# Spreading two small columns along rows: TensorE transposes, or a store and a broadcast load through DRAM

## The chip, the cores and the metric

The kernel runs on one core of one Trainium2 chip. The metric is the device time of one launch in microseconds (us); lower is better. The inputs and the output are those of the reference, in float32.

## What is computed

A decoder layer in three blocks, each followed by a layer norm: self-attention, a slot-attention block with a GRU cell, and a mixture of experts. The change lies in the second block. Its reference, cut down:

```python
# slots: (8, 256, 256), P: (8, 120, 256); k_proj, v_proj come from rmsnorm(P)
for _ in range(3):
    sn = slots * rsqrt(mean(slots * slots, axis=-1) + 1e-6) * w
    scores = einsum('bkd,bmd->bkm', sn @ Wq.T, k_proj) * D ** -0.5
    attn = softmax(scores, axis=-2)                      # over the 256 slots
    attn = attn / (sum(attn, axis=-1) + 1e-6)            # over the 120 context rows
    updates = einsum('bkm,bmd->bkd', attn, v_proj)
    slots = gru_cell(updates, slots, ...)
```

Two numbers per slot matter here: the **root** (the reciprocal root mean square of the slot, which scales its scores) and the **reciprocal of the column sum** (one over the sum of the slot's 120 attention weights).

## The kernel before

**Tiling.** There are 2048 slots in four groups of 512 (GT). Three iterations over four groups make STEPS = 12 steps, and each step handles one group. Slots lie transposed in SBUF, features on partitions and slots along the free dimension. Scores and attention weights have the 120 context rows on partitions and the 512 slots along the row. A step n has two halves, ch = 0 and 1, for the two 128-feature chunks of the hidden state.

**Why anything is spread.** Both per-slot numbers are made by matmuls with one output column (`squares`, L416, from the squared slots; `column_sums`, L1237, from the exponentials). They land as a 128x4 column block: slot t*128 + p on partition p, column t. They are used on 120 partitions with 512 slots along the row. `along_tokens` (L1210) does that turn: four TensorE transposes of a broadcast column against the identity put the 512 values on 120 partitions of a PSUM bank. `root_along(n)` (L1218) does it for the roots `rms` into bank 4, from which ScalarE copies them to `rr` (`rms_out`, L1362). `sums_along(n)` (L1249) does it for `crec` into bank 7, which VectorE reads directly.

**Order of the work.** It is written out by hand, one function per engine, and each engine runs its own list in order:

- TensorE (`slots_tensor`, L1217), for step n: r, z and n gates of half 0, then of half 1. A gate is six matmuls of 512 columns from the hidden state (`from_hidden`) and six of 256 columns from the update (`from_update`). The update of the r gate waits for the attention weights of the same step (`an_lo`). Between them stand `squares(n+2)` in `gates_n(n, 0)`, `column_sums(n+1)` in `gates_r(n, 1)`, and after `gates_z(n, 1)` the two spreads and `context_scores(n+2)`.
- ScalarE (`slots_scalar`, L1355): the tanh of the gates (`gate_r`, `gate_z`, `new`), `hidden_n`, `weights(n+1)` (the float16 copy of the attention weights), `rms_out(n+2)`, `squared_slots(n+3)`, `exponentials(n+2)`, `sums_high(n+3)`, `high_part(n+3)`.
- GpSimd (`slots_pool`, L1474): `slot_root(n+2)` (the power of -0.5), `difference` (old slots less candidate), `weights_low(n+1)`.
- VectorE (`slots_vector`, L1503), for step n: `reset(n,0)` L1553, `candidate(n,0)` L1561, `column_sums(n+1)` L1532 and L1536, `update(n,0)` L1568, `new_slots(n,0)` L1573, `weights(n+1)` L1546, `scaled_scores(n+2)` L1517, `reset(n,1)`, `candidate(n,1)`, `denominators(n+2)` L1527, `sums_low(n+3)` L1508, `low_part(n+3)` L441, `update(n,1)`, `mean_square(n+3)` L448, `new_slots(n,1)`.
- SyncE (`slots_sync`, L1451) issues nine loads at the start of the block and then nothing until the next block; it has no work while the steps run.

In step 10 the VectorE list differs: `weights(11)` stands before `update(10,0)`, behind four operations of the following layer norm (`norm_sum(0)`, L1085 to L1096).

Of the kernel before, what the change touches and what calls it, by code (L numbers as in the profile page):

```python
# [6 lines left out]
F32 = mybir.dt.float32  # L7
# [8 lines left out]
P = 128  # L16
# [18 lines left out]
def decoder_layer(nc, a, out):  # L35
# [23 lines left out]
    with top:  # L59
# [53 lines left out]
        PIECES = SHARED_PIECES + 4 * E  # L113
        halves = nc.dram_tensor("halves", [PIECES, P, 2 * I], F16, kind="Internal").ap()
# [257 lines left out]
        r_pow, rb_mm = sem("r_pow"), sem("rb_mm")  # L372
        h_hi, h_lo, h_sq, h_sum, ss_mm, r_msq = (sem(k) for k in ("h_hi", "h_lo", "h_sq", "h_sum", "ss_mm", "r_msq"))
# [3 lines left out]
        SQ_UP = 64.0  # L377

# [37 lines left out]
        def squares(n):  # L416
            if n < WHOLE:
                PE.wait_ge(h_sum, n + 1)
                if n == 0:
                    PE.wait_ge(vw_lo, 1)  # L420
                if n >= 1:
                    PE.wait_ge(r_msq, meaned(n - 1))
            else:
                PE.wait_ge(r_msq, squares_low(n))
                PE.wait_ge(h_sq, squares_high(n))
            if n >= 2:
                PE.wait_ge(c_eps2, n - 1)
# [29 lines left out]
        p_out = [sem(f"p_out{u}") for u in range(STAGED)]  # L457


        with ExitStack() as c:  # L460
# [20 lines left out]
            w_in = [sem(f"w_in{i}") for i in range(4)]  # L481
            x_in = [sem(f"x_in{i}") for i in range(3)]
# [700 lines left out]
        with ExitStack() as c:  # L1183
# [13 lines left out]
            warm_gelu = sb(c, "warm_gelu", [P, 1])[:, :]  # L1197
            tr_, tz, hn, t1, t2, nn, dl = (sb(c, k, [P, GT]) for k in ("tr_", "tz", "hn", "t1", "t2", "nn", "dl"))
# [11 lines left out]
            def along_tokens(bank, rows, column):  # L1210


                for t in range(TG):
                    mm = PE.transpose(ps[0:rows, bank, t * P:t * P + P], column[:, t:t + 1].broadcast_to((P, rows)), ident[:, :])
                return mm

            def slots_tensor():  # L1217
# [19 lines left out]
                def column_sums(n):  # L1237
                    PE.wait_ge(g_rec, n + 1)
                    if n + 1 < STEPS:
                        PE.wait_ge(r_msq, meaned(n + 1))  # L1240
                    if n >= 1:
                        PE.wait_ge(c_eps2, n)
                    for t in range(TG):
                        k = t * P // S
                        mm = PE.matmul(ps[:, 6, TG + t:TG + t + 1], exf[:, t * P:t * P + P], grec[0:M, k:k + 1],
                                       start=True, stop=True)
                    mm.then_inc(cs_mm, 1)

                def sums_along(n):  # L1249
                    PE.wait_ge(c_rec, n + 1)  # L1250
                    if n >= 1:
                        PE.wait_ge(an_out, BG * n)
# [17 lines left out]
                def gates_r(n, ch):  # L1270
# [8 lines left out]
                    if ch == 1 and n + 1 < STEPS:  # L1279
                        column_sums(n + 1)  # L1280
# [12 lines left out]
                def gates_n(n, ch):  # L1293
# [28 lines left out]
                for n in range(STEPS):  # L1322
# [3 lines left out]
                    if n == STEPS - 2:  # L1326
                        PE.wait_ge(rr_out, STEPS)
# [12 lines left out]
                    if n + 1 < STEPS:  # L1340
# [14 lines left out]
            def slots_scalar():  # L1355
# [67 lines left out]
                for n in range(STEPS):  # L1423
# [12 lines left out]
                    if n + 2 < STEPS:  # L1436
                        rms_out(n + 2)
# [13 lines left out]
            def slots_sync():  # L1451
# [10 lines left out]
                for q in range(SHARED_PIECES):  # L1462
                    SY.wait_ge(p_out[q % STAGED], 16 * (q // STAGED + 1))
                    SY.dma_start(sw_flat[:, 4 * I * (q // 2):4 * I * (q // 2 + 1)].rearrange("p (i c n) -> p i c n", i=2, c=2)[
                        :, :, q % 2, :], halves[q].rearrange("p (i n) -> p i n", i=2)).then_inc(sw_in, 16)

# [36 lines left out]
            def slots_vector():  # L1503
# [7 lines left out]
                def scaled_scores(n):  # L1511
                    VE.wait_ge(rr_out, n + 1)
# [16 lines left out]
                def column_sums(n):  # L1529

                    VE.wait_ge(cs_mm, n + 1)
                    VE.tensor_scalar(cse[:, :], ps[:, 6, TG:2 * TG], SUM_EPS, None, ALU.add).then_inc(c_eps2, 1)  # L1532
                    VE.wait_ge(c_eps2, n + 1)
                    if n >= 1:
                        VE.wait_ge(cb_mm, n)
# [108 lines left out]
        with ExitStack() as c:  # L1644
# [73 lines left out]
            gathered = [sem(f"gathered{q}") for q in range(NT // 2)]  # L1718
# [493 lines left out]
            def experts_tensor():  # L2212
# [49 lines left out]
                def add_sums():  # L2262

                    PE.wait_ge(made, 18)
                    for t in range(TG):
                        if t % CT == 0:
                            PE.wait_ge(gathered[(EARLY + t) // CT], 16)
# [153 lines left out]

            def combine_load(engine, q):

                rows = back_y[P + q * CT * P:P + (q + 1) * CT * P, :].rearrange("(t p) d -> p t d", p=P)
                engine.dma_start(xs[:, q * CT:(q + 1) * CT, :], rows).then_inc(gathered[q], 16)
# [25 lines left out]
            def combine_vector():  # L2451
                def statistics(tiles, done):
                    for t in tiles:
                        if t < EARLY and t % CT == 0:
                            VE.wait_ge(gathered[t // CT], 16)
# [82 lines left out]
```

## Time and profile before

| | |
|---|---|
| time, median of 3 runs (lowest to highest) | 886.9 us (886.7 to 887.6) |
| profiled execution, its own time | 890.64 us |
| span in that profile | 889.4 us |
| busy in the span: TensorE matmul, VectorE, ScalarE, GpSimd | 97%, 68%, 63%, 42% |
| granted TensorE clock, mean | 0.996 of full speed |
| attention block, slots block, experts | about 0 to 363 us, 363 to 560 us, 560 to 889 us |
| DMA traffic while the steps run (380 to 545 us) | at most 2 GB/s in the slices of 400 to 550 us |

The profile is one execution on the hardware profiler. Its time is 3.7 us above the median of the runs, so differences are worked out within it and then set against the median. "Busy" of TensorE is a modelled figure, since matmuls overlap; the start of each matmul is what to read. A row such as `dl<-slots,nn` names the written tile, then what is read.

### The profile page before, as it was taken

How to read it: one execution, taken by the hardware profiler on the slowest of the kernel's cores; microseconds unless marked ns; L12 is line 12 of the kernel's file. 1: busy time of each engine (PE TensorE's matmuls, PEld its weight loads, DVE VectorE, ACT ScalarE, POOL GpSimd, SP SyncE). 2: the span in 40 equal slices, each digit the busy share in tenths (PEclk: the TensorE clock that was granted, in tenths of full speed). 3: DMA queues.
4: the chain of work that ended last, by engine and by line, in shares of the span. 5: the costliest groups of instructions: out<-in, count | busy, mean ns of one | idle time of the engine just before them, and what ended most of it. 6: DMA issues, size and time to landing. Idle time of an engine off the chain costs nothing. (4 is left out here: it accounts for less than half of the span.)

```text
span 889.4 us, 23089 instructions
## 1 busy us (share of the span) xinstructions
PE 859.9 (97%) x8094; PEld 680.0 (76%) x8094; DVE 606.1 (68%) x1669; ACT 557.2 (63%) x1251; POOL 377.8 (42%) x492
## 2 busy tenths in 40 slices
PE   5999999999999999999999999999999999999996
PEld 3888788888888888767676666676788888887864
DVE  3667588776667675756666667869677767766655
ACT  4988776777676776655756565564455555555555
POOL 1634354343433475324444332544534444444433
PEclk9999999999999999999999999999999999999999
DMA  9733424342424331410000000399423323333226
GB/s 317 207 126 113 142 97 152 119 160 96 143 94 138 103 119 49 62 42 2 1 1 1 2 1 1 105 393 356 158 52 50 49 44 50 49 50 50 43 27 195
DMA packets 61579, 88.04 MB, mean 99 GB/s; under 512 B 17279, under 2 KB 46527, under 8 KB 61343
## 3 DMA queue, kind: packets, MB, share of 16 engines
q1 hardware_dynamic: 53439, 75.52, 25.8%
q0 software_dynamic: 7488, 10.27, 7.3%
q8 instruction: 71, 1.16, 0.6%
q10 hardware_dynamic: 544, 0.79, 0.3%
q14 instruction: 37, 0.30, 0.1%
HBM read 56.00 MB, written 30.56 MB: 97 GB/s over the span
## 5 line engine op out<-in xcount | busy, mean ns | idle before, releaser
L648 POOL TENSOR_SCALAR prob<-prob,rden 128x128 f32<-128x128 f32 (+1 forms) x256 | 122.9, 498 | 183.1 <-DVE rden L949 183.0
L2219 PE MATMUL ps<-slots,e 128*128 128x128 f16 x1872 | 190.0, 219 | 2.2 <-DVE xs L2386 2.1
L2219 PEld LDWEIGHTS ps<-slots,e 128*128 x1872 | 152.6, 97 | 35.3 <-issue 4.4
L843 ACT ACTIVATE prob<-prob,nmx 128x128 f32<-128x128 f32 (+1 forms) x256 | 113.2, 444 | 29.8 <-DVE nmx L943 29.8
L2227 PE MATMUL ps<-e,xT 128*128 x312 | 117.3, 378 | 0.0
L2316 ACT ACTIVATE slots<-slots 128x512 f32<-128x512 f32 x78 | 49.1, 630 | 106.8 <-DVE slots L2370 106.8
L943 DVE CUSTOM_DVE_ANT_0 prob<-ps,mask 128x128 f32<-128x128 f32 (+1 forms) x256 | 73.7, 353 | 41.5 <-PE ps L730 41.5
L31 PE MATMUL ps<-xT,wqkv 128*128 128x256 f16 x768 | 97.2, 278 | 2.0 <-ACT slots L850 1.4
L31 PEld LDWEIGHTS ps<-xT,wqkv 128*128 128x128 f16 x768 | 73.4, 99 | 18.3 <-issue 6.9
L1731 POOL DMA_INDIRECT xg<-rows_x,dst x39 | 40.9, 1049 | 106.3 <-DVE mask L2359 103.0
L2228 PE MATMUL ps<-e,xT 128*128 x312 | 85.0, 273 | 0.0
L2375 DVE TENSOR_TENSOR xT<-slots,xT 128x1024 f16<-128x1024 f32 x39 | 47.8, 1225 | 39.9 <-ACT xT L2322 39.9
L2191 POOL DMA_INDIRECT back_y<-xs,dst x39 | 62.2, 1595 | 29.8 <-DMA back_y<-xs,dst 16.7
L2370 DVE SCALAR_TENSOR_TENSOR slots<-ps,b1e 128x512 f32<-128x512 f32 x78 | 53.7, 691 | 26.5 <-PE ps L2219 26.3
L592 DVE SCALAR_TENSOR_TENSOR parted<-piece,parted 128x256 f16<-128x256 f32 x144 | 59.8, 463 | 0.0
L31 PE MATMUL ps<-an,wqkv 120*128 120x256 f16 x432 | 58.9, 272 | 0.5 <-POOL an L1477 0.5
L730 PE MATMUL ps<-slots 64*128 64x128 f32 (+1 forms) x512 | 53.1, 345 | 2.5 <-ACT slots L850 2.5
L31 PEld LDWEIGHTS ps<-an,wqkv 120*128 120x128 f16 x432 | 41.2, 99 | 16.5 <-POOL an L1477 2.5
L31 PE MATMUL ps<-wst,whh 128*128 128x512 f16 x216 | 52.5, 379 | 0.0
L31 PE MATMUL ps<-s,whh 128*128 128x512 f16 x216 | 52.5, 379 | 0.0
L956 DVE COPY pT<-ps 128x768 f32<-128x768 f32 x32 | 30.6, 956 | 31.8 <-PE ps L700 31.8
L741 PEld LDWEIGHTS ps<-pT,v 128*64 128x64 f32 x768 | 42.4, 139 | 11.5 <-issue 11.5
(267 smaller groups left out, 1855.3 us busy)
## 6 DMA issues: line engine op xcount, KB each, us to landing
halves<-parted SPq DMA_DIRECT2D x36, 512.0 KB, 2.9
piece<-in_L_ffn_ew SPq DMA_DIRECT2D x32, 512.0 KB, 4.5
e<-halves SPq DMA_DIRECT2D x16, 1024.0 KB, 15.2
piece<-in_L_ffn_sh_w SPq DMA_DIRECT2D x4, 512.0 KB, 8.8
sw<-halves SPq DMA_DIRECT2D x4, 512.0 KB, 6.8
rows_x<-xs SPq DMA_DIRECT2D x4, 512.0 KB, 7.4
xs<-back_y SPq DMA_DIRECT2D x8, 256.0 KB, 4.4
out<-xs SPq DMA_DIRECT2D x8, 256.0 KB, 2.1
```

The costliest lines, as they stand in the source:

```text
L31: mm = pe.matmul(out, w, x, start=first and n == 0, stop=last and n == len(products) - 1, **kw)
L592: VE.scalar_tensor_tensor(share(piece_part(q, 1)), share(like_part(q)), WS, share(piece_part(q, 0)), ALU.mult, ALU.subtract).then_inc(p_lo, 1)
L648: PO.tensor_scalar(prob[u][:, h, r], prob[u][:, h, r], rden[u][:, h, t:t + 1], 1.0, ALU.mult, ALU.mult).then_inc(normed, 1)
L730: mm = PE.matmul(ps[:, 2 + 2 * p + h, query_tile(t)], qk[p][r, 0, t * P:t * P + P], qk[p][r, 1, 0:(t + 1) * P], start=True, stop=True)
L843: SC.activation(at, at, ACT.Exp, bias=nmx[u][:, h, t:t + 1], scale=-1.0, accum_out=den[u][:, h, t:t + 1]).then_inc(exped, 1)
L943: VE.tensor_tensor_reduce(prob[u][:, h, r], ps[:, 2 + h, r], mask[:, r], -SCALE, HIGHEST, ALU.add, ALU.min, nmx[u][:, h, t:t + 1]).then_in ...
L2191: PO.indirect_dma_start(back_y, bass.IndirectOffsetOnAxis(ap=dst[:, i:i + 1], axis=0), yo[i % 2], None, compute_op=ALU.add).then_inc(rows_ ...
L2219: yield PE.matmul(ps[:, 2 * u + q, (k % 4) * P:(k % 4) * P + P], w[ch][h], xgT[u][j][:, ch, :], start=n == 0, stop=n == 3 * DC - 1)
L2227: yield PE.matmul(ps[:, 4 + u, :], he[u][0][:, k, :], w, start=k == 0, stop=False, skip_group_check=True)
L2228: yield PE.matmul(ps[:, 4 + u, 0:D], he[u][1][:, k, :], w[:, 0:D], start=False, stop=k == IC - 1, skip_group_check=True)
L2316: SC.activation(z, z, ACT.Gelu_apprx_tanh).then_inc(U_gelu, 1)
L2370: VE.scalar_tensor_tensor(z, ps[:, 2 * u + q, :].rearrange("p (k t) -> p k t", k=4), 1 / WS, bias, ALU.mult, ALU.add).then_inc(U_bias, 1)
```

## The change

The first two roots and the first column sums are still turned by transposes (ROOTS_TURNED = 2, SUMS_TURNED = 1). The ten later roots (n = 2 to 11) and eleven later column sums (n = 1 to 11) go through DRAM: SyncE stores the 128x4 block into a row of 512 floats and, when that store has landed, loads the row back to 120 partitions at once (a broadcast load). VectorE then reads `rr` and the new tile `cb` from SBUF. So that each partition stores two neighbouring floats instead of four scattered ones, the slots are given to partitions in another way (`paired`): the weights of the one-column matmuls are read with a step of two elements. `column_sums(n+1)` moves from `gates_r(n, 1)` into `gates_n(n, 0)` on TensorE, ahead of `squares(n+2)`, and its result goes to bank 7. ScalarE's `rms_out(n+2)` goes away for n + 2 from 2 on. The combine loads of the last block use semaphores again that the first block had used, and wait for 32 instead of 16 where they do.

```diff
+        root_row = nc.dram_tensor("root_row", [GT], F32, kind="Internal").ap()
+        sums_row = nc.dram_tensor("sums_row", [GT], F32, kind="Internal").ap()
...
+        ROOTS_TURNED, SUMS_TURNED = 2, 1
+        def paired(t):
+            return t.rearrange("p (k q j) -> p k j q", k=BG, j=TG // BG)
...
                     for i in range(2):
-                        mm = PE.matmul(ps[:, 6, t:t + 1], sqh[i][:, t * P:t * P + P], one_h, start=i == 0,
+                        mm = PE.matmul(ps[:, 6, t:t + 1], paired(sqh[i][:, :])[:, t // BG, t % BG, :], one_h, start=i == 0,
...
         def slot_root(n):
             PO.wait_ge(r_msq, meaned(n))
-            if n >= 1:
+            if 1 <= n <= ROOTS_TURNED:
                 PO.wait_ge(rb_mm, n)
+            elif n > ROOTS_TURNED:
+                PO.wait_ge(root_put, 16 * (n - ROOTS_TURNED))
...
                 def column_sums(n):
                     PE.wait_ge(g_rec, n + 1)
...
                     for t in range(TG):
-                        k = t * P // S
-                        mm = PE.matmul(ps[:, 6, TG + t:TG + t + 1], exf[:, t * P:t * P + P], grec[0:M, k:k + 1],
-                                       start=True, stop=True)
+                        k = t // BG
+                        weights = exf[:, t * P:t * P + P] if n < SUMS_TURNED else paired(exf)[:, k, t % BG, :]
+                        mm = PE.matmul(sums_of(n)[:, t:t + 1], weights, grec[0:M, k:k + 1], start=True, stop=True)
...
                     from_hidden(n, 0, ch, False)
-                    if ch == 1 and n + 1 < STEPS:
-                        column_sums(n + 1)
                     PE.wait_ge(an_lo, n + 1)
...
                     from_hidden(n, 2, 2 * DC + ch, True).then_inc(hn_mm, 1)
+                    if ch == 0 and n + 1 < STEPS:
+                        column_sums(n + 1)
                     if ch == 0 and n + 2 < STEPS:
                         squares(n + 2)
...
-                    if n + 1 < STEPS:
-                        sums_along(n + 1)
                     if n + 2 < STEPS:
-                        root_along(n + 2)
                         context_scores(n + 2)
...
-                    if n + 2 < STEPS:
-                        rms_out(n + 2)
                     hidden_n(n, 1)
...
+                def token_pairs(row):
+                    return row.rearrange("(k q j) -> q k j", k=BG, j=TG // BG)
+                def put_sums(n):
+                    SY.wait_ge(c_rec, n + 1)
+                    if n > SUMS_TURNED:
+                        SY.wait_ge(sums_in, 16 * (n - SUMS_TURNED))
+                    SY.dma_start(token_pairs(sums_row), crec[:, :].rearrange("p (k j) -> p k j", k=BG)).then_inc(sums_put, 16)
...
+                def spread_sums(n):
+                    SY.wait_ge(sums_put, 16 * (n - SUMS_TURNED + 1))
+                    SY.wait_ge(an_out, BG * n)
+                    SY.dma_start(cb[0:M, :], sums_row.rearrange("(o t) -> o t", o=1).broadcast_to((M, GT))).then_inc(
+                        sums_in, 16)
...
+                for n in range(STEPS):
+                    if n + 1 < STEPS:
+                        put_sums(n + 1)
+                    if n + 2 < STEPS:
+                        put_root(n + 2)
+                    if n + 1 < STEPS:
+                        spread_sums(n + 1)
+                    if n + 2 < STEPS:
+                        spread_root(n + 2)
...
                 def weights(n):
-                    VE.wait_ge(cb_mm, n + 1)
+                    if n < SUMS_TURNED:
+                        VE.wait_ge(cb_mm, n + 1)
+                    else:
+                        VE.wait_ge(sums_in, 16 * (n - SUMS_TURNED + 1))
...
-                        VE.scalar_tensor_tensor(an[0:M, cols], ex[0:M, k, :], grec[0:M, k:k + 1], ps[0:M, 7, cols],
+                        VE.scalar_tensor_tensor(an[0:M, cols], ex[0:M, k, :], grec[0:M, k:k + 1],
+                                                ps[0:M, 7, cols] if n < SUMS_TURNED else cb[0:M, cols],
```

`put_root` and `spread_root` are built like `put_sums` and `spread_sums`, on `r_pow`, `root_in`, `root_put` and `sc_out`. VectorE's `scaled_scores(n)` waits for `root_in`, and its reciprocal L1536 for `sums_put` of the step before.

**How the instructions move.** TensorE in step 1 of the program before, from the column sums to the scores (`grec,ex` are the column sums of step 2, `ident,crec` and `ident,rms` the two spreads, `s,kq` the scores of step 3; `wst,whh` is a hidden-state gate, `an,wqkv` an update gate):

```order
806 L1245 MATMUL ps<-grec,ex 128x1 [waits c_eps2,r_msq,g_rec]
807 L1245 MATMUL ps<-grec,ex 128x1 x3
808 L31 MATMUL ps<-an,wqkv 128x256 [waits an_lo]
809 L31 MATMUL ps<-an,wqkv 128x256 x5
810 L31 MATMUL ps<-wst,whh 128x512 [waits tz_out]
811 L31 MATMUL ps<-wst,whh 128x512 x5
812 L31 MATMUL ps<-an,wqkv 128x256 x6
813 L1214 MATMUL ps<-ident,crec 120x128 [waits an_out,c_rec]
814 L1214 MATMUL ps<-ident,crec 120x128 x3
815 L1214 MATMUL ps<-ident,rms 120x128 [waits rr_out,r_pow]
816 L1214 MATMUL ps<-ident,rms 120x128 x3
817 L31 MATMUL ps<-s,kq 120x256 [waits sc_out,h_hi,h_lo]
818 L31 MATMUL ps<-s,kq 120x256 x11
```

In the changed program the column sums stand ahead of the squares (`one_f,sqs`), in the same step:

```order
796 L1264 MATMUL ps<-grec,ex 128x1 [waits c_eps2,g_rec]
797 L1264 MATMUL ps<-grec,ex 128x1 x3
798 L442 MATMUL ps<-one_f,sqs 128x1 [waits h_sq,r_msq]
799 L442 MATMUL ps<-one_f,sqs 128x1 x7
800 L31 MATMUL ps<-an,wqkv 128x256 [waits t2_out]
```

and the stretch from the update of the r gate to the next gate is:

```order
804 L31 MATMUL ps<-an,wqkv 128x256 [waits an_lo]
805 L31 MATMUL ps<-an,wqkv 128x256 x5
806 L31 MATMUL ps<-wst,whh 128x512 [waits tz_out]
807 L31 MATMUL ps<-wst,whh 128x512 x5
808 L31 MATMUL ps<-an,wqkv 128x256 x6
809 L31 MATMUL ps<-s,kq 120x256 [waits sc_out,h_hi,h_lo]
810 L31 MATMUL ps<-s,kq 120x256 x11
811 L31 MATMUL ps<-wst,whh 128x512 [waits hn_out]
```

The two spreads are gone between the z gate and the scores, and the column sums come one r gate earlier, right behind the hidden part of the n gate. SyncE's list behind the loads of the block, where the program before goes on with the stores and loads of the next block (`sums_row` and `root_row` are the two rows in DRAM):

```order
99 L1485 DMA sums_row<-crec 128x2x2 [waits c_rec]
100 L1491 DMA root_row<-rms 128x2x2 [waits r_pow]
101 L1496 DMA cb<-sums_row 120x512 [waits an_out,sums_put]
102 L1502 DMA rr<-root_row 120x512 [waits sc_out,root_put]
103 L1485 DMA sums_row<-crec 128x2x2 [waits sums_in,c_rec]
104 L1491 DMA root_row<-rms 128x2x2 [waits root_in,r_pow]
```

There are 42 such transfers, four per step and two in the last, each load behind its own store. VectorE's list keeps its order; only its waits change:

```order
917 L1583 TENSOR_SCALAR cse<-ps 128x4 [waits cs_mm]
918 L1589 RECIPROCAL crec<-cse 128x4 [waits sums_put,c_eps2]
919 L1625 SCALAR_TENSOR_TENSOR dl<-tz,dl 128x512 [waits tz_out,dl_out]
920 L1630 SCALAR_TENSOR_TENSOR slots<-dl,nn 128x512 [waits u_out]
921 L1602 SCALAR_TENSOR_TENSOR an<-ex,grec,cb 120x256 [waits an_hi,an_lo,g_rec,sums_in]
922 L1602 SCALAR_TENSOR_TENSOR an<-ex,grec,cb 120x256
923 L1568 ISA sc,gmx<-ps,rr 120x256 [waits g_exp,sc_mm,root_in]
```

Two operations stand between the reciprocal and the weights that use it, as before.

## Rows read from the trace of the kernel before

**Rows 1.** Page, part 1: busy time, share of the span, instructions.

```profile
PE 859.9 (97%) x8094; PEld 680.0 (76%) x8094; DVE 606.1 (68%) x1669; ACT 557.2 (63%) x1251; POOL 377.8 (42%) x492
```

**Rows 2.** Stretches: busy us of five engines, granted clock, DMA share, GB/s.

```profile
5.00:10.00 5.00, 2.20 (x8) 1.42 (x8) 1.53 (x2) 2.51 (x3) 0.00 (x0) 1.00 1.04 382
...
475.00:490.00 15.00, 14.88 (x109) 10.20 (x108) 9.81 (x22) 9.35 (x18) 6.41 (x5) 1.00 0.00 0
```

**Rows 3.** VectorE, timeline of steps 1 to 9: start us, duration, line, [idle before].

```profile
403.83 0.18 DVE L1536 RECIPROCAL crec<-cse 128x4 f32<-128x4 f32 x1
...
407.19 0.87 DVE L1546 SCALAR_TENSOR_TENSOR an<-ex,grec,ps 120x256 f32<-120x256 f32 x2
409.23 0.42 DVE L1517 CUSTOM_DVE_ANT_0 sc<-ps,rr 120x256 f32<-120x256 f32 x1 [1.17 <-ACT rr L1366]
...
412.92 1.35 DVE L1508 SCALAR_TENSOR_TENSOR sqs<-wst,sqs 128x512 f16<-128x512 f32 x1 [1.01 <-ACT sqs L1360]
...
525.51 0.18 DVE L1536 RECIPROCAL crec<-cse 128x4 f32<-128x4 f32 x1
```

**Rows 4.** TensorE, timeline of the same steps.

```profile
401.75 0.95 PE L1245 MATMUL ps<-grec,ex 120*128 120x1 f32 x8
...
405.17 0.60 PE L1214 MATMUL ps<-ident,crec 128*120 128x128 f32 x4
405.61 0.60 PE L1214 MATMUL ps<-ident,rms 128*120 128x128 f32 x4
406.04 1.47 PE L31 MATMUL ps<-s,kq 128*120 128x256 f16 x12
...
410.60 0.82 PE L31 MATMUL ps<-an,wqkv 120*128 120x256 f16 x6
...
416.66 0.95 PE L1245 MATMUL ps<-grec,ex 120*128 120x1 f32 x8
```

**Rows 5.** Waits from 380 to 545 us: total us, times, longest.

```profile
PEld ps L433 <- DVE sqs L1508: 4.2, 7, 0.7
```

**Rows 6.** ScalarE and GpSimd, timeline of step 1, second half.

```profile
408.09 0.62 ACT L1380 CAST an<-an 120x512 f16<-120x512 f32 x1 [0.76 <-DVE an L1546]
408.62 0.58 ACT L1366 COPY rr<-ps 120x512 f32<-120x512 f32 x1
409.10 0.69 ACT L1403 ACTIVATE hn<-ps,bhh 128x512 f32<-128x512 f32 x1
...
411.65 0.72 ACT L1352 ACTIVATE nn<-t,bih 128x512 f32<-128x512 f32 x1
...
408.80 1.16 POOL L1477 TENSOR_TENSOR an<-an 120x512 f16<-120x512 f32 x1 [0.99 <-ACT an L1380]
```

**Rows 7.** DMA issues: count, KB each, median us from issue to landing.

```profile
out<-xs SPq DMA_DIRECT2D x8, 256.0 KB, 2.1
...
b2s<-in_L_ffn_sh_b SPq DMA_DIRECT2D x1, 128.0 KB, 3.7
...
gw<-in_L_ffn_gate_w SPq DMA_DIRECT2D x1, 8.0 KB, 2.2
gb<-in_L_ffn_gate_b SPq DMA_DIRECT2D x1, 4.0 KB, 2.6
b1s<-in_L_ffn_sh_b SPq DMA_DIRECT2D x1, 4.0 KB, 2.5
```

**Rows 8.** VectorE and ScalarE, timeline of step 0 and of step 10.

```profile
388.02 0.18 DVE L1536 RECIPROCAL crec<-cse 128x4 f32<-128x4 f32 x1
...
391.03 0.87 DVE L1546 SCALAR_TENSOR_TENSOR an<-ex,grec,ps 120x256 f32<-120x256 f32 x2
...
393.94 0.69 ACT L1403 ACTIVATE hn<-ps,bhh 128x512 f32<-128x512 f32 x1 [0.90 <-PE ps L31]
...
539.73 0.18 DVE L1536 RECIPROCAL crec<-cse 128x4 f32<-128x4 f32 x1
...
543.09 0.87 DVE L1546 SCALAR_TENSOR_TENSOR an<-ex,grec,ps 120x256 f32<-120x256 f32 x2
```

More of the change, by code:

```diff
@@ L372, in decoder_layer @@
         r_pow, rb_mm = sem("r_pow"), sem("rb_mm")
+        root_put, root_in, sums_put, sums_in = (sem(k) for k in ("root_put", "root_in", "sums_put", "sums_in"))
         h_hi, h_lo, h_sq, h_sum, ss_mm, r_msq = (sem(k) for k in ("h_hi", "h_lo", "h_sq", "h_sum", "ss_mm", "r_msq"))
@@ L425, in squares @@
                 PE.wait_ge(h_sq, squares_high(n))
-            if n >= 2:
-                PE.wait_ge(c_eps2, n - 1)
+            if n == 2:
+                PE.wait_ge(c_eps2, 1)
             for t in range(TG):
@@ L452, in slot_root @@
             PO.wait_ge(r_msq, meaned(n))
-            if n >= 1:
+            if 1 <= n <= ROOTS_TURNED:
                 PO.wait_ge(rb_mm, n)
+            elif n > ROOTS_TURNED:
+                PO.wait_ge(root_put, 16 * (n - ROOTS_TURNED))
             PO.tensor_tensor(rms[:, :], msq[:, :], powh[:, 0:TG], ALU.pow).then_inc(r_pow, 1)
         p_out = [sem(f"p_out{u}") for u in range(STAGED)]
+        loaded = [sem(f"loaded{q}") for q in range(NT // 2)]
+        w_in, x_in = loaded[0:4], loaded[4:7]
         with ExitStack() as c:
@@ L1215, in along_tokens, with sums_of @@
                 return mm
+            def sums_of(n):
+                return ps[:, 6 if n < SUMS_TURNED else 7, TG:2 * TG]
             def slots_tensor():
@@ L1326, in slots_tensor @@
                     if n == STEPS - 2:
-                        PE.wait_ge(rr_out, STEPS)
+                        PE.wait_ge(rr_out, ROOTS_TURNED)
                         PE.wait_ge(sc_out, BG * STEPS)
@@ L1511, in scaled_scores @@
                 def scaled_scores(n):
-                    VE.wait_ge(rr_out, n + 1)
+                    if n < ROOTS_TURNED:
+                        VE.wait_ge(rr_out, n + 1)
+                    else:
+                        VE.wait_ge(root_in, 16 * (n - ROOTS_TURNED + 1))
                     VE.wait_ge(sc_mm, n + 1)
@@ L1531, in column_sums @@
                     VE.wait_ge(cs_mm, n + 1)
-                    VE.tensor_scalar(cse[:, :], ps[:, 6, TG:2 * TG], SUM_EPS, None, ALU.add).then_inc(c_eps2, 1)
+                    VE.tensor_scalar(cse[:, :], sums_of(n), SUM_EPS, None, ALU.add).then_inc(c_eps2, 1)
                     VE.wait_ge(c_eps2, n + 1)
-                    if n >= 1:
-                        VE.wait_ge(cb_mm, n)
+                    if n == SUMS_TURNED:
+                        VE.wait_ge(cb_mm, SUMS_TURNED)
+                    elif n > SUMS_TURNED:
+                        VE.wait_ge(sums_put, 16 * (n - SUMS_TURNED))
                     VE.reciprocal(crec[:, :], cse[:, :]).then_inc(c_rec, 1)
                 def weights(n):
-                    VE.wait_ge(cb_mm, n + 1)
+                    if n < SUMS_TURNED:
+                        VE.wait_ge(cb_mm, n + 1)
+                    else:
+                        VE.wait_ge(sums_in, 16 * (n - SUMS_TURNED + 1))
                     VE.wait_ge(g_rec, n + 1)
@@ L1717, in decoder_layer @@
                 sem(k) for k in ("U_mm", "U_bias", "U_gelu", "U_hi", "U_lo", "D_mm", "D_out"))
-            gathered = [sem(f"gathered{q}") for q in range(NT // 2)]
             f_stat, f_rstd, f_norm, f_late, stored = (
@@ L2419, in late_low, with combine_loaded @@
                 VE.tensor_tensor(hh[m % 3][1], hf[m % 2], hh[m % 3][0], ALU.subtract).then_inc(H_late, 1)
+            def combine_loaded(engine, q):
+                engine.wait_ge(loaded[q], 32 if q < len(w_in) + len(x_in) else 16)
             def combine_load(engine, q):
                 rows = back_y[P + q * CT * P:P + (q + 1) * CT * P, :].rearrange("(t p) d -> p t d", p=P)
-                engine.dma_start(xs[:, q * CT:(q + 1) * CT, :], rows).then_inc(gathered[q], 16)
+                engine.dma_start(xs[:, q * CT:(q + 1) * CT, :], rows).then_inc(loaded[q], 16)
             def combine_sync():
```

22 lines of the change are left out of this document (15 added, 7 removed).

## The prediction

> **What bounds the kernel now.** I read the page's shares first, then the stretches, then the timelines of one step, then the waits. TensorE is busy 97% of the span [rows 1] and nearly all of a 15 us stretch of the steps [rows 2], so at first sight 84 transposes fewer should shorten the kernel. The timeline says otherwise. The reciprocal of the column sums, once per step on VectorE, starts at 403.83 in step 1 and at 525.51 in step 9 [rows 3]: eight periods of 15.21 us. TensorE's own work per step is less, 14.91 us from one `column_sums` to the next in step 1 to 2, where it was catching up [rows 4]. Later it waits seven times for VectorE's `sums_low` ahead of `squares` [rows 5]. The pace of steps 1 to 9 is that of a chain over VectorE, ScalarE and GpSimd, and TensorE follows it by a hair.
>
> That chain, in step 1: the reciprocal ends at 404.01, the weights start at 407.19 [rows 3], ScalarE copies them at 408.09, copies the roots at 408.62, makes `hn` at 409.10 and comes to `nn` at 411.65, with its work back to back [rows 6]. `sums_low` follows at 412.92, after a wait for ScalarE, and the next reciprocal one period after the last [rows 3].
>
> **What is removed.** Per step two groups of four transposes: 405.17 to 405.61 and 405.61 to 406.04, 0.44 and 0.43 us [rows 4]; ten times both and once the first, 9.1 us of TensorE. Since TensorE waits for the chain, this gives nothing by itself. It leaves TensorE 14.91 - 0.87 = 14.04 us per step. ScalarE's copy of the roots goes too: 0.48 us from its start to the start of `hn` [rows 6], and that lies in the chain. VectorE's wait of 1.17 us ahead of the scores was for this copy [rows 3]. Gain: **0.48 us per step**, as `nn` is then 0.48 earlier and so is `sums_low`.
>
> **What is added.** The weights now wait for the reciprocal to go to DRAM and back: store, landing, broadcast load, landing. Call the time from the end of the reciprocal to the landing of the load **L**. The slack is what the transposes never used: 407.19 - 404.01 = 3.18 us, in which VectorE waits for GpSimd and does `update` and `new_slots`. What L has beyond 3.18 delays the weights, and behind them on VectorE stand the scores, `reset`, `candidate` and all the rest of the chain. From the start of the weights to the end of the next reciprocal it takes 15.21 - 3.18 = 12.03 us, 11.55 without the copy. The new period is L + 11.55, and a step costs **L - 3.66**.
>
> L is not in the trace; its bounds are the short DMAs of SyncE's queue [rows 7]. Store, 256 runs of 8 bytes: 2.2 us (`gw`, 8 KB) to 2.5 (`b1s`, 1024 runs of 4 bytes); I take 2.3, nearer to the first since it has a quarter of the runs. Load, 120 partitions by 2 KB of one row, 240 KB: at least 2.1 (`out`, 256 KB, no broadcast). The broadcasts took 2.6 (4 KB) and 3.7 (128 KB). If what 3.7 has above 2.2 grew with the bytes, it would be 1.5 x 240 / 128 = 2.8, a load of 5.0. I take 3.0: `out` shows that 256 KB cost little, and `b2s` was issued behind the 1024 short runs of `b1s`. Three hand-offs between engines at 0.03 each (the weights end at 408.06, ScalarE starts at 408.09 [rows 3, 6]) make 0.1. **L = 2.3 + 3.0 + 0.1 = 5.4**, with ends at 2.2 + 2.1 = 4.3 and 2.5 + 5.0 + 0.1 = 7.6.
>
> The Trainium skill (DMA: Bandwidth & Descriptors, Anatomy of one DMA) gives about 2.0 us fixed per DMA plus bytes over 436 GB/s, fitted on another issuing path; by it L would be an estimated 4.6 and the time some 897 us. The same page (Specifications) says that runs below 512 bytes are read, modified and written, which speaks against this store; no row here shows such a store alone.
>
> **The sum.** Steps 1 to 9: 9 x (L - 3.66). Step 0: the reciprocal ends at 388.20; `hn` started at 393.94 and waited for TensorE [rows 8]. Now `hn` starts 0.90 + 0.52 after the weights, at 389.62 + L, so the step costs L - 4.32. Step 10: the slack is again 543.09 - 539.91 = 3.18 [rows 8], now four layer-norm operations, and no root copy is saved: L - 3.18. Together 11 L - 40.44, at L = 5.4 **+19.0 us**. The profiled execution took 890.6, 3.7 above the median; its like would be 909.6. Against the median: 886.9 + 19.0 = **905.9 us**.
>
> **Edits costed at nothing.** The roots take the same way, one issue behind (0.4 to 0.5 us) on SyncE. The scores started 2.42 us before `nn` (409.23, 411.65 [rows 3, 6]); the new `nn` is due 3.98 after the weights (4.46 less 0.48). So the roots may land 1.56 us after the sums unseen; beyond that each tenth costs a tenth per step. The read of the weights with a step of two, the other place of the column sums and the later `xn` lie on TensorE, which now idles: its r update needs `an_lo`, which GpSimd finishes 408.80 + 1.16 - 407.19 = 2.77 us after the weights [rows 6], where before TensorE came at 3.41 [rows 4]. With a period of 16.95 and 14.04 of work it idles 2.9 us per step. Were the chain ever to wait for TensorE, dearer weight loads would show. What the weights read from SBUF instead of PSUM I leave at the same price. SyncE has nothing else queued during the steps, and its later transfers wait for the end of the last steps anyway, so they move with them.
>
> **Rivals.**
> 1. *Both transfers at their shortest* (L 4.3 to 4.7): +6.9 to +11.3, 893.8 to 898.2. For it: the DMA engines are idle here [rows 2]. Against: the store is of scattered short runs, the load a broadcast. 0.14.
> 2. *A slow load or store* (L 6.2 to 7.6): +27.8 to +43.2, 915 to 930. For it: the 3.7 of `b2s`. 0.16.
> 3. *Faster: both trips hidden in the slack.* The store and the load land before `new_slots` is done; it decides at L = 3.66, 1.8 us for each transfer. With L under 3.18, nine steps gain 0.48 and step 0 up to 0.87 (TensorE's), 881.7 us; if TensorE were the pace after all, 9.1 us go, 877.8. For it: 97% busy TensorE [rows 1]. Against: no row of SyncE's queue is below 2.1, so two make 4.2 [rows 7], and the 15.21 period against 14.91. The Trainium skill (DMA: Bandwidth & Descriptors, Latency and other measured facts) puts the least round trip of a tiny transfer at about 800 ns; by it the store alone would be an estimated 1.5 us shorter than I take. 0.08.
> 4. *TensorE's clock falls in the new gaps.* At 1.2 instead of 2.4 GHz, 14.04 us of work become up to 28, 11 us more per step, over 1000 us in all. For it: a gap of 2.9 us each step, where there was none. Against: with TensorE busy 2.20 of 5 us the granted clock was 1.00, the upper level [rows 2]. 0.02.
>
> That the change does not do what it says can be left out: the transposes are gone from TensorE's list.
>
> **How the numbers follow.** My forecast, L from 4.7 to 6.2, has 0.58; the likeliest value in it is the prediction. The range takes in most of rivals 1 and 2: from 893 (L just under 4.3) to 924 (L = 7.0). Faster by over 0.2%, about what a measurement of this kernel tells from no change: 0.08, rival 3. Within 0.2% (L near 3.7): 0.02. Slower: 0.90.
>
> **What would show it.** Right: the period of the reciprocals near 17 us; VectorE's longest new wait ahead of the weights (for a DMA), about 2.2 us, ten times; TensorE's idle time ahead of the r update, released by GpSimd's `an_lo`, over 2 us per step; no wait ahead of the scores; before 380 us and after the slots block nothing moved but the start. Each DMA's time from issue to landing gives L directly. Wrong: a period at or below 15.2, or VectorE's wait ahead of the scores instead of the weights (then the roots are the slow ones), or a period of over 17 with L below 5.4 (then the chain has a link that I missed).

## The result and the profile after

The changed kernel takes **943.1 us** (median; 942.1 to 946.7), against 887.2 for the kernel before on the same chip: a ratio of 1.0623, 95% interval 1.0601 to 1.0644. It is slower, as forecast, but by 56 us and not by 19; 943.1 lies outside the range of 893 to 924. The profiled execution took 943.9 us. One of the ten executions of the first run below took 1777.2 us, twice the others, and stays out of its ratio; why is open.

| | before | after |
|---|---|---|
| median, us | 887.2 | 943.1 |
| span of the profiled execution, us | 889.4 | 942.7 |
| mean granted TensorE clock | 0.996 | 0.967 |
| reciprocal of step 1 to reciprocal of step 10, us | 135.90 (9 x 15.10) | 180.60 (9 x 20.07) |

The busy times of the page hardly move, and the stretch of the steps is where they thin out: TensorE's busy time rose by 13 us although 84 transposes went away, which answers to [rows 1].

```profile
span 942.7 us, 22962 instructions
PE 872.8 (93%) x8010; PEld 679.3 (72%) x8010; DVE 613.6 (65%) x1669; ACT 554.2 (59%) x1241; POOL 380.9 (40%) x492
...
PE   5999999999999999887778888899999999999996
...
PEclk9999999999999999999977888899999999999999
```

Fewer matmuls with more busy time point to a slower clock: the granted-clock row has 7s and 8s in the middle of the span, where it had 9s throughout.

VectorE's timeline of steps 3 and 4 (start us, duration, line, operation, [idle before]) answers to [rows 3]; the first and last rows are the reciprocals of steps 1 and 10:

```profile
404.78 0.18 DVE L1589 RECIPROCAL crec<-cse 128x4 f32<-128x4 f32 x1
...
443.32 0.18 DVE L1589 RECIPROCAL crec<-cse 128x4 f32<-128x4 f32 x1
...
450.84 0.88 DVE L1602 SCALAR_TENSOR_TENSOR an<-ex,grec,cb 120x256 f32<-120x256 f32 x2 [4.01 <-DMA cb<-sums_row]
...
460.49 0.16 DVE L457 TENSOR_SCALAR msq<-ps 128x4 f32<-128x4 f32 x1 [1.09 <-PE ps L442]
...
462.74 0.18 DVE L1589 RECIPROCAL crec<-cse 128x4 f32<-128x4 f32 x1
...
585.38 0.18 DVE L1589 RECIPROCAL crec<-cse 128x4 f32<-128x4 f32 x1
```

From the reciprocal's end, 443.50, to the weights, 450.84, it is 7.34 us, where it was 3.18. VectorE stands idle for 4.01 of them, until the load of `cb` lands. The eleven steps have 7.14 to 7.76 here, 7.38 in the mean.

SyncE's queue for the same trip, and the landing times from 380 to 600 us (count, KB each, median us from issue to landing), answer to [rows 7]:

```profile
443.53 0.38 SPq L1485 DMA_DIRECT2D sums_row<-crec  x1
444.00 0.42 SPq L1491 DMA_DIRECT2D root_row<-rms  x1
447.00 0.34 SPq L1496 DMA_DIRECT2D cb<-sums_row  x1
448.23 0.34 SPq L1502 DMA_DIRECT2D rr<-root_row  x1
```

```profile
cb<-sums_row SPq DMA_DIRECT2D x11, 240.0 KB, 4.1
rr<-root_row SPq DMA_DIRECT2D x10, 240.0 KB, 3.7
sums_row<-crec SPq DMA_DIRECT2D x11, 2.0 KB, 3.3
root_row<-rms SPq DMA_DIRECT2D x10, 2.0 KB, 4.2
```

The load is issued 3.47 us after the store (447.00 less 443.53) and the weights start 3.84 after that. So the trip is 3.5 + 3.8: a store of 2 KB takes almost as long as a load of 240 KB.

The waits from 375 to 640 us (total us, times, longest):

```profile
DVE an L1602 <- DMA cb<-sums_row: 44.9, 11, 4.5
...
PE ps L31 <- POOL an L1525: 40.6, 11, 5.0
...
DVE msq L457 <- PE ps L442: 16.9, 9, 3.5
...
DVE sc L1568 <- DMA rr<-root_row: 1.5, 2, 1.0
```

The wait for `cb` is passed on: VectorE waits 44.9 us for the DMA, GpSimd for ScalarE's copy of the weights (73.4 us, where it was 27.6 before), TensorE 40.6 us for GpSimd's `an_lo`. The roots are waited for twice, 1.5 us in all. The fourth row was not forecast: VectorE waits for TensorE's `squares`. TensorE's own rows show why. Its timeline of step 3, and below it stretches (busy us of five engines, granted clock, DMA share, GB/s):

```profile
448.72 1.46 PE L31 MATMUL ps<-wst,whh 128*128 128x512 f16 x6
453.67 0.83 PE L31 MATMUL ps<-an,wqkv 120*128 120x256 f16 x6 [3.49 <-POOL an L1525]
454.34 2.51 PE L31 MATMUL ps<-wst,whh 128*128 128x512 f16 x6
```

```profile
455.00:456.00 1.00, 1.00 (x4) 0.39 (x3) 0.09 (x2) 0.94 (x2) 0.51 (x2) 0.50 0.08 16
...
458.00:459.00 1.00, 1.00 (x6) 0.46 (x5) 1.00 (x2) 0.00 (x0) 0.00 (x0) 1.00 0.00 0
430.00:450.00 20.00, 15.57 (x100) 9.94 (x100) 10.92 (x21) 9.15 (x16) 7.44 (x7) 0.91 0.16 29
490.00:510.00 20.00, 16.58 (x100) 10.39 (x100) 10.88 (x21) 9.26 (x16) 6.46 (x5) 0.83 0.10 22
```

After 3.49 us without work the granted clock is 0.50 at 455, the lower level of 1.2 GHz, and six matmuls of 512 columns take 2.51 us instead of 1.46. By 458 it is 1.00 again. Over 20 us that makes 0.91 in the early steps and 0.83 in the later ones; in [rows 2] it was 1.00. Not every such gap is followed by a fall: behind 3.50 us without work, which end at 415.13 in step 1, the clock stays at 1.00.

### The profile page after: what moved, and what is told of

It reads as the page before. It is cut to its first block and busy times, and to the rows that moved or that the text cites. A ratio compares the mean times of both kernels' runs of the same rounds, so it can differ in the third digit from the quotient of the medians.

```text
span 942.7 us, 22962 instructions
## 1 busy us (share of the span) xinstructions
PE 872.8 (93%) x8010; PEld 679.3 (72%) x8010; DVE 613.6 (65%) x1669; ACT 554.2 (59%) x1241; POOL 380.9 (40%) x492
## 5 line engine op out<-in xcount | busy, mean ns | idle before, releaser
L31 PE MATMUL ps<-an,wqkv 120*128 120x256 f16 x432 | 68.8, 302 | 40.6 <-POOL an L1525 40.6
L31 PEld LDWEIGHTS ps<-an,wqkv 120*128 120x128 f16 x432 | 44.6, 107 | 67.1 <-POOL an L1525 46.0
L2247 POOL DMA_INDIRECT back_y<-xs,dst x39 | 63.0, 1615 | 30.2 <-DMA back_y<-xs,dst 12.7
L31 PE MATMUL ps<-wst,whh 128*128 128x512 f16 x216 | 59.0, 414 | 0.0
L31 PE MATMUL ps<-s,whh 128*128 128x512 f16 x216 | 59.0, 414 | 0.0
L752 PE MATMUL ps<-pT,v 128*64 128x128 f32 x768 | 49.0, 277 | 0.8 <-ACT v L874 0.8
```

Of the source, the lines that this page charges most:

```text
L31: mm = pe.matmul(out, w, x, start=first and n == 0, stop=last and n == len(products) - 1, **kw)
L2247: PO.indirect_dma_start(back_y, bass.IndirectOffsetOnAxis(ap=dst[:, i:i + 1], axis=0), yo[i % 2], None, compute_op=ALU.add).then_inc(rows_ ...
```

## The experiments

Three theories. **A**: the weights wait for the trip through DRAM, and each step costs the trip less its slack (the prediction's chain), with a slower TensorE clock on top. **B**: TensorE itself got slower (stepped weight reads, the moved column sums). **C**: the 42 transfers slow the engines down by their traffic. The kernel before took 888.5 to 888.8 us beside these runs, and the differences below are against it. Times of trips and periods are from each run's timeline of VectorE.

### The transfers without the wait

The kernel before, with all 42 transfers added on SyncE (the roots into a tile `rr2`); nobody waits for what they load.

```diff
+                for n in range(STEPS):
+                    if n + 1 < STEPS:
+                        put_sums(n + 1)
+                    if n + 2 < STEPS:
+                        put_root(n + 2)
...
+                    if n > SUMS_TURNED:
+                        VE.wait_ge(sums_put, 16 * (n - SUMS_TURNED))
                     VE.reciprocal(crec[:, :], cse[:, :]).then_inc(c_rec, 1)
```

> The kernel before with all 42 transfers added, each behind its own store as in the change, but with all transposes kept and nobody waiting for a load to land (only the next reciprocal and the next root wait until their store has landed). Theory A (the weights wait for the trip through DRAM, beyond a slack of 3.18 us per step): as before, 886 to 889 us, period 15.2 us, and the trip is still some 7.4 us long. Theory B (the loss is TensorE's: weights read with a step of two, other places of its work): as before too. Theory C (the transfers themselves, or SyncE issuing them, slow the other engines): slower by a large part of 56 us.

888.8 us, ratio 1.0004 (0.9992 to 1.0016): no difference, and two neighbouring reciprocals stand 15.21 us apart. Theory C falls: the traffic costs nothing that can be measured here. The transfers take nearly what they take in the changed kernel, 4.1 and 3.3 there (landing times as above):

```profile
cb<-sums_row SPq DMA_DIRECT2D x11, 240.0 KB, 4.0
...
sums_row<-crec SPq DMA_DIRECT2D x11, 2.0 KB, 3.0
```

### One wait more

```diff
                     VE.wait_ge(cb_mm, n + 1)
+                    if n >= SUMS_TURNED:
+                        VE.wait_ge(sums_in, 16 * (n - SUMS_TURNED + 1))
```

> The same, and VectorE's weights wait for the landing of the load as well; transposes, ScalarE's root copy and all layouts as before. Theory A: the period is L + 12.0, with L = 7.4 as in the changed kernel 19.4 us; the sum over the steps is 11 L - 35.6 = +46 us, so 933 us, up to 10 more if TensorE's clock falls in its gap of 4.5 us. Theory B: within 3 us of the kernel before, since TensorE's work is untouched. Theory C: as e1.

936.6 us, ratio 1.0545 (1.0526 to 1.0563). All transposes, the copy and the old weight reads are still there, and a single wait brings 48 of the 56 us. Theory B is not needed for them. The trip is 7.37 us in the mean of steps 1 to 9, the period 19.39. From the start of the weights to the end of the next reciprocal it is 12.02 or 12.03 us in seven of steps 1 to 8 (13.13 in step 2, where the clock is at 0.50 for over 6 us), and the prediction's chain says 12.03. From the waits:

```profile
DVE an L1603 <- DMA cb<-sums_row: 45.9, 11, 4.8
```

### The change with its TensorE gap filled

The changed kernel with 18 more matmuls of 512 columns in steps 1 to 10, where TensorE would idle; nobody reads what they compute.

```diff
                     from_hidden(n, 0, ch, False)
+                    if ch == 0 and 1 <= n < STEPS - 1:
+                        for q in range(FILL):
+                            PE.matmul(ps[:, 4, :], whh[0][:, 0, 0:P], sh[n % NG][0][:, 0, :], start=True, stop=True,
+                                      skip_group_check=True)
                     PE.wait_ge(an_lo, n + 1)
```

> The changed kernel with 18 matmuls of 512 columns more ahead of the r update of half 0 in steps 1 to 10, into a bank that nobody reads: 3.9 us of work in a gap of 5 us. Theory A with its second part (TensorE's clock falls to 1.2 GHz after the gap, its squares come late and VectorE waits for them): the granted clock stays at 1.00, the period goes from 20.4 to 18.9, VectorE's wait ahead of the mean square goes, 887.2 + 11 x 7.4 - 40.4 = 928 us. If the clock is only a side show: 943 us. Theory B with busy TensorE as the bound: slower than 943, by up to 39 us.

930.5 us, ratio 1.0494 (1.0449 to 1.0539): **12.7 us less than the change, with 180 matmuls more**. The interval is 4 us wide either way, since one of the four executions took 936.5. In the filled steps the clock no longer falls, and of VectorE's nine waits for `squares`, 16.9 us, two are left, 4.0 us. A stretch of 40 us, then the first and the last of ten reciprocals:

```profile
470.00:510.00 40.00, 38.19 (x248) 23.49 (x249) 23.20 (x45) 20.17 (x38) 14.46 (x12) 1.00 0.13 26
```

```profile
402.27 0.18 DVE L1596 RECIPROCAL crec<-cse 128x4 f32<-128x4 f32 x1
...
573.54 0.18 DVE L1596 RECIPROCAL crec<-cse 128x4 f32<-128x4 f32 x1
```

From step 1 to step 10 it is 171.27 us, 19.03 per step, with a mean trip of 7.41. In the change it is 180.60, so the fallen clock costs 1.04 us per step there, 9.3 in nine steps, though its idle TensorE hides most of the slower matmuls. The other 3.3 of the 12.7 us lie outside these nine steps. From the weights to the end of the next reciprocal it is 11.78 us, where the prediction has 11.55; in the change 11.78 to 12.08 in steps 1 to 3 and about 13 from step 4 on.

### The roots alone, the sums alone

Each half of the change alone. The roots through DRAM, the sums still transposed:

```diff
+                    if n < ROOTS_TURNED:
+                        VE.wait_ge(rr_out, n + 1)
+                    else:
+                        VE.wait_ge(root_in, 16 * (n - ROOTS_TURNED + 1))
```

> The roots alone through DRAM, the column sums by transposes and in their old place. The root is made some 5 us before the weights, so its trip of 7.4 us lands at about 409.8 on the time scale of the profile before, 2.6 us after the weights start and 1.0 beyond what is free; ScalarE's copy of 0.48 us goes. Theory A: +0.5 us per step, 887 to 893 us, VectorE waiting ahead of the scores for the load. Theory B: TensorE has 0.43 us less per step, 883 us, or slower if the stepped read costs.

The sums through DRAM, the roots still transposed:

```diff
+                    if n < SUMS_TURNED:
+                        VE.wait_ge(cb_mm, n + 1)
+                    else:
+                        VE.wait_ge(sums_in, 16 * (n - SUMS_TURNED + 1))
```

> The column sums alone through DRAM; the roots by transposes with ScalarE's copy, column sums in their old place on TensorE. Theory A (the weights' wait is the loss): as e2, which had the same wait and all the transposes: 933 to 937 us, period L + 12.0. Theory D (part of L comes from the two pairs of transfers sharing SyncE and the DMA engines): L falls from 7.4 to 6.5 or less, and the time to 926 us or less. TensorE's 0.44 us less per step gives nothing.

The roots alone: 894.3 us, ratio 1.0069 (1.0050 to 1.0088). The sums alone: 932.7, ratio 1.0512 (1.0477 to 1.0547). The sums carry the loss. Without the roots' transfers beside it their trip is 7.03 us in the mean of steps 1 to 9, so sharing the queue costs 0.35 of the 7.4. The weights wait 41.8 us for it in all.

The roots are not free when alone. They are read ten times with a wait of 1.5 us, more than the 1.17 us of before for ScalarE's copy, and some periods grow from 15.3 to 16.6. From the waits:

```profile
DVE sc L1563 <- DMA rr<-root_row: 14.9, 10, 1.8
...
PEld ps L442 <- DVE sqs L1551: 12.8, 8, 2.1
```

The trace shows which steps grow. In step 6 `reset` on VectorE starts together with a GpSimd operation and takes 1.81 us instead of 0.69, and `nn` on ScalarE then waits 1.42 us for VectorE:

```profile
487.00 1.81 DVE L1599 SCALAR_TENSOR_TENSOR t<-tr_,hn 128x512 f32<-128x512 f32 x1
487.00 1.27 POOL L423 TENSOR_TENSOR wst<-wst 128x512 f32<-128x512 f32 x1 [0.37 <-ACT wst L416]
```

All five long steps have such a row (`reset` twice; `gneg`, the negated maxima of the scores, three times, 1.03 to 1.21 us instead of 0.17), and the four short ones have none. So the late roots push VectorE's next operations into GpSimd's. In the whole change this trip hides behind that of the sums (1.5 us of wait in all).

### The row in SBUF instead of DRAM

The sums alone again, the row kept on one partition of SBUF. The store is split in two, one for each of the two 256-slot halves.

```diff
+                    for k in range(BG):
+                        SY.dma_start(row_s[0:1, k * S:(k + 1) * S].rearrange("o (q j) -> o q j", j=2),
+                                     crec[:, 2 * k:2 * k + 2].unsqueeze(1)).then_inc(sums_put, 16)
...
+                    SY.dma_start(cb[0:M, :], row_s[0:1, :].unsqueeze(1).broadcast_to((1, M, GT))).then_inc(
+                        sums_in, 16)
```

> As e5, but the row of 512 stands on one partition of an SBUF tile instead of in DRAM: two stores (one for each half of the row, 0.4 us more of issue) and a load that reads that partition 120 times. If writing to DRAM and reading it back is what makes the trip long: L of 6 us or less, 920 us or less. If any pair of DMAs behind one another costs this: L 7.4 to 7.8, 935 to 940 us. If 120 reads of one partition are slow: longer still.

1011.8 us, ratio 1.1402 (1.1371 to 1.1433). The store got cheaper, the load far dearer (landing times from 380 to 600 us, then VectorE's timeline):

```profile
cb<-row_s SPq DMA_DIRECT2D x9, 240.0 KB, 10.8
row_s<-crec SPq DMA_DIRECT2D x18, 1.0 KB, 2.0
```

```profile
438.47 0.18 DVE L1583 RECIPROCAL crec<-cse 128x4 f32<-128x4 f32 x1
...
452.09 0.88 DVE L1596 SCALAR_TENSOR_TENSOR an<-ex,grec,cb 120x256 f32<-120x256 f32 x2 [10.91 <-DMA cb<-row_s]
```

A trip of 13.4 us: 10 us more of trip per step than the slack, and 123 us more in the kernel, with the mean granted clock at 0.943. It is a third point for theory A, in the wrong direction for a repair. The 128 runs of 8 bytes land in 2.0 us in SBUF, and 256 of them in 2.9 to 3.3 in DRAM; how much of the difference is the number of runs and how much the place, this pair does not separate.

### The copy of the roots moved, no DMA

The kernel before with `root_along` ahead of `gates_z(n, 1)` and `rms_out` ahead of `gate_z(n, 1)`, in ScalarE's idle time: the 0.48 us that the prediction gave to the missing copy, without any DMA.

```diff
+                    if n + 2 < STEPS:
+                        rms_out(n + 2)
                     gate_z(n, 1)
                     if n + 1 < STEPS - 1:
                         weights(n + 1)
-                    if n + 2 < STEPS:
-                        rms_out(n + 2)
```

> The kernel before, no DMA: the transposes of the roots one z gate earlier on TensorE, and ScalarE's copy of the roots ahead of the tanh of the z gate, where it idles 1.6 us per step. This takes the 0.48 us out of the chain that the change also took out. Theory A: the chain's period would be 14.7, TensorE's work of 14.91 becomes the bound, so nine steps gain 0.3: 884 to 885 us, 3 us less than before. Theory B or no chain: no change.

887.5 us, ratio 0.9995 (0.9985 to 1.0006): no difference, and the expected 884 to 885 was too low. The period did fall, from 15.21 to 14.90, to where TensorE is busy all of the time (VectorE's timeline, then a stretch):

```profile
401.92 0.18 DVE L1537 RECIPROCAL crec<-cse 128x4 f32<-128x4 f32 x1
...
416.82 0.18 DVE L1537 RECIPROCAL crec<-cse 128x4 f32<-128x4 f32 x1
```

```profile
440.00:480.00 40.00, 40.00 (x298) 28.18 (x297) 27.36 (x54) 25.09 (x44) 16.88 (x13) 1.00 0.00 1
```

The copy did lie in the chain, as the prediction said. Behind it stands TensorE's own work, 14.91 us [rows 4], so only 0.3 of the 0.48 could come out. Eight such steps make 2.5 us, which would lie outside the interval (1.3 us less to 0.5 more). In the traces 1.9 us are left from the reciprocal of step 0 to the last weights (153.13 against 155.07), since the last period got longer, 14.64 against 14.22; and what follows takes 1.2 us more (347.46 against 346.31).

### The trip started earlier

The sums alone through DRAM, with `column_sums` and its reciprocal moved earlier in the step (behind the hidden part of the z gate, half 0, and ahead of `low_part`), the roots by transposes with their copy moved as above.

```diff
                     from_hidden(n, 1, DC + ch, False)
+                    if ch == 0 and n + 1 < STEPS:
+                        column_sums(n + 1)
...
                         sums_low(n + 3)
+                    if n + 2 < STEPS:
+                        column_sums(n + 2)
+                    if n + 3 < STEPS:
                         low_part(n + 3)
```

> Column sums through DRAM as in the change, but made one r gate and two z gates earlier: on TensorE between the two parts of the z gate of half 0, on VectorE right behind sums_low of the step before. The reciprocal then ends some 7.8 us before the weights could start, and a trip of 7.0 to 7.5 us hides. Roots by transposes, with the copy moved as in e7. Theory A: no wait for the load ahead of the weights, the period 14.7, TensorE's work 14.5: 882 to 884 us. If L is over 7.8 here, each tenth costs 1 us.

889.0 us, ratio 1.0008 (0.9996 to 1.0020). No row shows a wait for `cb`. The reciprocal ends at 442.43, the weights start at 450.58, 8.15 us later, and the trip disappears in them (VectorE's timeline):

```profile
442.25 0.18 DVE L1584 RECIPROCAL crec<-cse 128x4 f32<-128x4 f32 x1
...
450.58 0.88 DVE L1597 SCALAR_TENSOR_TENSOR an<-ex,grec,cb 120x256 f32<-120x256 f32 x2
```

Same transfers, same reads from SBUF, same stepped weights as with the sums alone, and 43.7 us less (the moved copy alone brought nothing, above). It isn't the DRAM row that costs, but where in the step it begins. But nothing is won on the kernel before either: the period is 15.2 again, and the expected 882 to 884, with a period of 14.7, were missed by 5. The moved column sums and their reciprocal now stand in VectorE's chain, between `sums_low` and `low_part`, which starts 1.55 us after it (456.00, 457.55) instead of 1.26 in the run with the copy moved; that 0.29 is about what the moved copy had gained.

Then the same move in the changed kernel, both rows through DRAM:

> The whole change, with only column_sums(n+1) and its reciprocal made earlier in the step (behind the hidden part of the z gate, first half, on TensorE; ahead of low_part on VectorE). Both rows still go through DRAM. Theory A (the price is what the trip of the sums has beyond its slack): reciprocal to weights about 8 us, of which the trip needs some 7.3, so no wait for cb, period 15.2 to 15.4 as in the run with the sums alone moved, the clock at 1.00 all through, and the roots the only trip left to see (e4 saw up to 1.4 us per step in some steps): 888 to 896. Rival C (42 transfers on the queue hold each other or the engines up, wherever they start): periods above 17 and over 905. Rival B (the stepped reads of squares and weights make TensorE slower): TensorE work per step above 14.5 us without any gap.

899.8 us, ratio 1.0131 (1.0109 to 1.0152), 43 us less than the change, and 4 us above the upper end of what was expected. The column sums are hidden in nine of eleven steps; the roots are what is left (the waits, then SyncE's queue):

```profile
DVE sc L1568 <- DMA rr<-root_row: 12.9, 10, 2.2
...
DVE an L1602 <- DMA cb<-sums_row: 1.4, 2, 0.9
```

```profile
445.89 0.38 SPq L1485 DMA_DIRECT2D sums_row<-crec  x1
449.23 0.38 SPq L1491 DMA_DIRECT2D root_row<-rms  x1
449.70 0.42 SPq L1496 DMA_DIRECT2D cb<-sums_row  x1
452.13 0.34 SPq L1502 DMA_DIRECT2D rr<-root_row  x1
```

The roots of that step are made at 447.51 by VectorE and GpSimd and leave at 449.23; their load is due 3.9 us after 452.13, and the scores start at 456.11. SyncE's order matters too: the load of `cb` stands behind the roots' store, which waits for GpSimd. The store of the sums, 3.0 us from 445.89, had landed by 448.9.

## Why the prediction was wrong in size

**Right.** The direction, the place and the form. Transposes on TensorE were worth nothing; VectorE's new wait stands ahead of the weights, eleven times and not ten, for 4.1 us and not 2.2; it is passed on to TensorE's r update, 3.7 us each time (over 2 was said); the scores wait next to never; the transfers' traffic costs nothing. With the copy the chain's arithmetic holds to a few hundredths of a microsecond: from the start of the weights to the end of the next reciprocal it was to be 12.03, and 11.55 without the copy. Trip and period are means of steps 1 to 9, and the last column is the median of steps 1 to 8 (the period into step 10, whose list differs, is shorter: 14.22 before).

| kernel | trip | period | period less trip | weights to next reciprocal |
|---|---|---|---|---|
| before | 3.19 | 15.10 | 11.91 | 12.01 |
| one wait more | 7.37 | 19.39 | 12.02 | 12.03 |
| sums alone | 7.03 | 18.95 | 11.92 | 12.04 |
| the change, gap filled | 7.41 | 19.03 | 11.62 | 11.78 |
| the change | 7.39 | 20.07 | 12.68 | 12.96 |

**The step that failed: the size of L.** It was put together as 2.3 + 3.0 + 0.1 = 5.4 from [rows 7]; it measures 7.38. The store takes 3.3 instead of 2.3, the load some 4 instead of 3.0. The upper ends (2.5 for the store, 5.0 for the load) add up to a value that holds the result, but the store alone lies outside its own bounds: all rows taken for it were loads, except `out`, which is 256 KB. No small store stood in the trace, and a load of 8 KB was allowed to stand in for one. By the prediction's own formula L = 7.38 gives 11 x 7.38 - 40.44 = +40.7 us instead of +19.0: 21.7 of the 37 us missing. The Trainium skill (DMA: Bandwidth & Descriptors, Anatomy of one DMA) would have given 4.6 and 897 us, an estimate for another issuing path; it is farther off than the rows were.

**The second: rival 4, given 0.02.** The clock fell, for 9.3 us in nine steps and 12.7 in the whole kernel (the change against the run with the gap filled). The rival had its mechanism right and both its weights wrong. Its price, 11 us per step, took all of the step's work at half speed; the rows show 0.83 to 0.91 of full clock, and a TensorE with spare time in the step absorbs most of it. What argued against it was a row of 5 us with TensorE busy for 2.20 and a clock of 1.00 [rows 2]. That row was misread, because its clock column does not fit the matmuls. In the kernel before, the same twelve matmuls take 2.72 us at 10.5 and 1.49 at 19.3, under a clock column of 1.00 from 0 to 40 us:

```profile
10.53 2.72 PE L31 MATMUL ps<-xT,wqkv 128*128 128x256 f16 x12 [0.56 <-DVE wqkv L931]
19.31 1.49 PE L31 MATMUL ps<-xT,wqkv 128*128 128x256 f16 x12
```

So TensorE was slow there too, and the row was no evidence against the rival. A longer trip also feeds it: at the forecast L the gap would have been shorter. In the run with one wait more, which still has the transposes, TensorE waits 34.6 us for `an_lo` instead of 40.6, and the mean clock is 0.980 instead of 0.967. The length of one gap does not decide alone: there 2.35 us without work, ending at 396.38, were followed by 0.50, and 2.64 us, ending at 456.17, by 1.00. What does decide was not tried.

**The third, small: the gain of 0.48 from the missing copy.** In the filled run it is 0.25, 12.03 less 11.78. `nn` starts 4.22 us after the weights in step 3 of the change, not 3.98, and it waits for VectorE:

```profile
455.06 0.72 ACT L1365 ACTIVATE nn<-t,bih 128x512 f32<-128x512 f32 x1 [0.16 <-DVE t L1618]
```

Before, VectorE waited for the copy until GpSimd's `an_lo` was nearly done; now `gneg` or `reset` falls into it and takes up to 1.2 us (last section). The rows show this; no run takes it apart.

**The sum.** From the reciprocal of step 0 to the last weights the traces have 155.07 us (388.02 to 543.09) and 207.49 (385.43 to 592.92), 52.4 more. The trip gives 40.7 of it and the clock 9.3. Another 1.8 in steps 1 to 9 is about what the copy's smaller gain makes (9 x 0.23 = 2.1), and step 0 has the last 0.6. The spans differ by 53.3: 2.6 us less ahead of this stretch and 3.5 more behind it. Between the forecast's base of 886.9 and the median it is 56.2. These 2.6, 3.5 and the last 2.9 us are not explained.

**Costed at nothing.** Rightly: stepped weight reads, reads of `cb` from SBUF, the other bank, the traffic. The roots' trip was hidden in this change only because that of the sums is longer; alone it costs 0.7%.

## What to carry over

Price a trip through DRAM as a small store plus a load, each from its own kind of row: here 3.0 to 3.3 us for 2 KB out and 4.0 for 240 KB back, 7.0 to 7.4 us from operand to operand. Compare that with the slack between producer and consumer, and if it is longer, start it earlier in the step or leave it: beyond the slack every tenth is paid every step. Then look at the gap that the wait opens on TensorE in each step, since the matmuls behind it may run at half clock, as here behind most such gaps but not all. And check a clock column against the time that the same matmuls take elsewhere before it is used as evidence.

## What was not expected of the hardware

- **Matmuls that nobody reads made the kernel 12.7 us faster**; the granted clock stayed at 1.00 from 385 to 560 us.
- **Broadcasting 2 KB from one SBUF partition to 120 took 10.8 us**, from a DRAM row 4.0 to 4.1 for the same 240 KB. Why was not tried.
- **Some operations of VectorE last longer beside one of GpSimd.** `gneg`, 120x2 elements, took 0.17 us in the kernel before and 1.09 in step 3 of the change:

```profile
452.46 1.16 POOL L1525 TENSOR_TENSOR an<-an 120x512 f16<-120x512 f32 x1 [6.09 <-ACT an L1393]
452.55 1.09 DVE L1572 TENSOR_SCALAR gneg<-gmx 120x2 f32<-120x2 f32 x1
```

GpSimd's `an_lo` ran from 452.46 to 453.62, and `gneg` ended at 453.64. In the run with the sums alone moved earlier it was `reset` (1.11 us instead of 0.69, from 437.60), beside a GpSimd operation that ended at 438.15; `reset` ended 0.56 later. The Trainium skill (SBUF — State Buffer, SBUF: two separate sides) says that the two engines share one pair of SBUF ports, for certain operations of VectorE (in a 2-port mode, or with two inputs from SBUF) against those of GpSimd, and that whichever starts first holds it for the whole instruction while the other is blocked. Both rows agree: each VectorE operation started behind GpSimd's. The price, up to 1.0 us per `gneg` in the change, is not all free: it stands ahead of `nn` where the missing copy gave 0.25 us and not 0.48, and with the roots alone each of the five steps that had it took 1.2 to 1.4 us more.
